# Attention value products of two key tiles by turns: four halves between changes of PSUM bank

## What is computed

```python
def _L0_attn_ref(x, query_proj, key_proj, value_proj, output_proj):
    q = jnp.einsum('bnd,hkd->bnhk', x, query_proj)
    k = jnp.einsum('bnd,hkd->bnhk', x, key_proj)
    v = jnp.einsum('bnd,hvd->bnhv', x, value_proj)
    sim = jnp.einsum('bnkh,bmhk->bnhm', q, k)
    attn = jax.nn.softmax(sim * scale, axis=1)
    o = jnp.einsum('bnhm,bmhv->bnhv', attn, v)
    return jnp.einsum('bnhv,dhv->bnd', o, output_proj)
```

## Time and profile before

| | before |
|---|---|
| median of 3 runs | 1898.89 us |
| profiled execution | 1899.13 us |
| its span | 1897.8 us |
| TensorE matmul busy | 1781.7 us (94%) |
| VectorE busy | 1708.0 us (90%) |
| ScalarE busy | 1397.8 us (74%) |
| value products (L535), time on the chain that ended last | 50% of the span |
| row maxima (L942) | 1024 of 1221 ns mean |
| exponentials (L708) | 1024 of 1113 ns mean, and 193 ns each for the row sum's read |
| value matmuls (L535) | 8192 of 614 ns mean |

### The profile page before, as it was taken

The page is one execution under the profiler, slowest core; times in us unless marked ns, Lnnn a source line. Parts: engine busy times, 40 slices in busy tenths (PEclk is TensorE's granted clock), DMA queues, the critical chain, the costliest instruction groups (busy, mean ns, idle before and its releaser), DMA issues.

```text
span 1897.8 us, 38562 instructions
## 1 busy us (share of the span) xinstructions
PE 1781.7 (94%) x15122; PEld 821.9 (43%) x15122; DVE 1708.0 (90%) x2369; ACT 1397.8 (74%) x2554; POOL 501.6 (26%) x976
## 2 busy tenths in 40 slices
PE   6969999999999999896999999999999989999996
PEld 5732222222222222581222222222222278899995
DVE  6959999999999999467999999999999789999995
ACT  3349999999999999346999999999999723222222
POOL 2002212221122112101112211221122436565664
PEclk9979999999999999997999999999999999999998
DMA  4110011110011100311111100111000222222200
GB/s 164 45 67 29 29 32 37 35 40 29 30 37 37 40 29 13 99 67 51 32 38 37 38 29 30 37 36 40 29 29 29 96 94 68 67 70 68 70 12 17
DMA packets 52980, 89.05 MB, mean 47 GB/s; under 512 B 3264, under 2 KB 35392, under 8 KB 52800
## 3 DMA queue, kind: packets, MB, share of 16 engines
q1 hardware_dynamic: 52112, 85.01, 13.9%
q10 hardware_dynamic: 688, 1.58, 0.2%
HBM read 57.21 MB, written 29.36 MB: 46 GB/s over the span
## 4 chain that ended last, share of the span: by engine, by line
PE 77%; DVE 13%; issue 3%; ACT 3%; DMA 2%; POOL 1%; SPq 0%; ACTq 0%; DVEq 0%; POOLq 0%
PE acc L535 50%; PE slot L506 11%; PE slot L390 6%; PE acc L390 5%; PE acc L552 4%; DVE nm L942 4%; ACT e_sb L708 2%; DMA stk<-qk_parts 1%; DVE e_sb L1023 1%; PE slot L593 1%; DVE ost L953 1%; DVE e_sb L1022 1%; DVE e_sb L1018 1%; DVE qx L1014 0%; DVE e_sb L1044 0%
## 5 line engine op out<-in xcount | busy, mean ns | idle before, releaser
L942 DVE TENSOR_REDUCE nm<-slot 128x1 f32<-128x1024 f32 x1024 | 1208.3, 1221 | 30.6 <-PE slot L506 25.1
L708 ACT ACTIVATE e_sb<-slot,nm 128x1024 f32<-128x1024 f32 x1024 | 1140.0, 1113 | 79.7 <-DVE nm L942 65.7
L535 PE MATMUL acc<-e_sb,vp 64*64 64x512 f32 x8192 | 1118.1, 614 | 27.8 <-DVE ost L953 15.2
L535 PEld LDWEIGHTS acc<-e_sb,vp 64*64 64x64 f32 x8192 | 228.5, 131 | 591.8 <-issue 315.1
L506 PE MATMUL slot<-stq,stk 64*64 64x512 f16 x4096 | 427.5, 385 | 36.9 <-DMA stk<-qk_parts 22.5
L506 PEld LDWEIGHTS slot<-stq,stk 64*64 64x64 f16 x4096 | 138.7, 107 | 370.9 <-ACT e_sb L708 253.4
L1169 POOL TENSOR_TENSOR dlt<-nm 128x4 f32<-128x4 f32 x128 | 25.5, 199 | 747.0 <-DVE nm L942 747.0
L708 ACT ACTIVATION_READ_ACCUMULATOR e_sb<-slot,nm 128x1 f32 x1024 | 197.4, 193 | 0.0
L1160 POOL TENSOR_TENSOR vp<-v_sb,fac 128x512 f32<-128x512 f32 x128 | 133.4, 1042 | 10.0
L791 POOL TENSOR_TENSOR hqT_lo<-e_sb,hqT_hi 128x640 fp32r<-128x640 f32 x64 | 117.8, 1861 | 50.8 <-ACT hqT_hi L642 50.8
L744 ACT COPY e_sb<-slot 128x256 f32<-128x256 f32 x32 | 11.9, 373 | 160.8 <-PE slot L563 160.8
(11 more groups left out here) (195 smaller groups left out, 1797.2 us busy)
## 6 DMA issues: line engine op xcount, KB each, us to landing
stk<-qk_parts SPq DMA_DIRECT2D x128, 128.0 KB
o_heads<-ost SPq DMA_DIRECT2D x64, 256.0 KB, 3.2
v_sb<-o_heads SPq DMA_DIRECT2D x8, 2048.0 KB, 8.3
qk_parts<-e_sb SPq DMA_DIRECT2D x32, 256.0 KB, 2.1
stq<-qk_parts SPq DMA_DIRECT2D x128, 64.0 KB
v_sb<-in_x SPq DMA_DIRECT2D x12, 512.0 KB, 9.2
out<-e_sb SPq DMA_DIRECT2D x32, 128.0 KB, 1.7
e_sb<-in_x SPq DMA_DIRECT2D x4, 512.0 KB, 10.0
```

The lines of the kernel that those rows point to most:

```text
L535: mm = pe.matmul(acc[half * VD:(half + 1) * VD, c * 512:(c + 1) * 512], vp[rows, g % 3, gi, half, :], e_v[rows, j % ERING, n0:n0 + 512], s ...
L708: act.activation(e_v[:, j % ERING, half * 1024:(half + 1) * 1024], slot[u % 3][:, :], ACT.Exp, bias=nm[:, g % 4, i, half:half + 1], accum_ ...
L942: dve.tensor_reduce(nm[:, g % 4, i, half:half + 1], slot[u % 3][:, :], AX.X, ALU.max, negate=True).then_inc(maxed.sem)
```

## The change

`attend` takes the value products of two key tiles together, in four steps: step 0 is one half of tile 2p, step 1 the half of tile 2p+1 with the same bank for each row tile; in step 2 the row tiles change banks and the other half of tile 2p follows, step 3 is that of tile 2p+1. The next pair begins with the banks that step 3 had. So the one wait of TensorE for its own earlier work is in step 2, for step 1. `attended` of tile 2p is signalled at the end of step 2, a step later than before; that of tile 2p+1 where it was. The wait for `vp` stands once for four tiles. Each step has the matmuls of a turn before.

```diff
-        def attend(b, j, turn):
+        def attend(b, n):
+            pair, step = divmod(n, 4)
+            j = 2 * pair + step % 2
+            last = step >= 2
             h, i = divmod(j, NT)
             g, gi = divmod(j, GROUP)
-            if turn == 0:
+            if step == 0 and gi == 0:
                 pe.wait_ge(*vp_made.past(b * JG + g))
-            if turn == 0 and i == 0 and h:
+            if step == 0 and i == 0 and h:
                 pe.wait_ge(*took_low.past(b * H + h - 1))
                 pe.wait_ge(*took_high.past(b * H + h - 1))
...
-            if turn == 1:
-                pe.wait_ge(*half_attended.past(b * JT + j))
-            elif j:
-                pe.wait_ge(*attended.past(b * JT + j - 1))
+            if step == 2:
+                pe.wait_ge(*half_attended.past(b * JT // 2 + pair))
             for side in range(2):
-                c = turn ^ side
+                c = (pair + last + side) % 2
                 rows = slice(side * 64, side * 64 + 64)
                 for half in range(2):
                     n0 = half * 1024 + c * 512
                     mm = pe.matmul(acc[half * VD:(half + 1) * VD, c * 512:(c + 1) * 512], vp[rows, g % 3, gi, half, :],
-                                   e_v[rows, j % ERING, n0:n0 + 512], start=(i == 0 and turn == 0),
-                                   stop=(i == NT - 1 and turn == 1))
-            mm.then_inc((attended if turn else half_attended).sem)
+                                   e_v[rows, j % ERING, n0:n0 + 512], start=(i == 0 and not last),
+                                   stop=(i == NT - 1 and last))
+            if step == 1:
+                mm.then_inc(half_attended.sem)
+            if last:
+                mm.then_inc(attended.sem)
...
-                            attend(b, j - LAG, half)
+                            attend(b, 2 * (j - LAG) + half)
```

More of the change, by code:

```diff
@@ L509, in scores @@
             mm.then_inc(scored.sem)
-        def attend(b, j, turn):
+        def attend(b, n):
+            pair, step = divmod(n, 4)
+            j = 2 * pair + step % 2
+            last = step >= 2
             h, i = divmod(j, NT)
             g, gi = divmod(j, GROUP)
-            if turn == 0:
+            if step == 0 and gi == 0:
                 pe.wait_ge(*vp_made.past(b * JG + g))
-            if turn == 0 and i == 0 and h:
+            if step == 0 and i == 0 and h:
                 pe.wait_ge(*took_low.past(b * H + h - 1))
                 pe.wait_ge(*took_high.past(b * H + h - 1))
-            elif turn == 0 and i == 0:
-                last = len(uses[b]) - 1
-                for t in range(last - 3, last + 1):
+            elif step == 0 and i == 0:
+                final = len(uses[b]) - 1
+                for t in range(final - 3, final + 1):
                     if t % 4 >= 2:
                         pe.wait_ge(*quarter_read(b, t))
-            if turn == 1:
-                pe.wait_ge(*half_attended.past(b * JT + j))
-            elif j:
-                pe.wait_ge(*attended.past(b * JT + j - 1))
+            if step == 2:
+                pe.wait_ge(*half_attended.past(b * JT // 2 + pair))
             for side in range(2):
-                c = turn ^ side
+                c = (pair + last + side) % 2
                 rows = slice(side * 64, side * 64 + 64)
```

## The result

The changed kernel takes 1830.83 us (median of 4 runs, 1828.42 to 1833.94) against 1899.7 us for the kernel before (median of 4 runs): a ratio of 0.9641, 95% interval 0.962 to 0.9662. The forecast was 1831. The profiled execution took 1828.42 us, span 1827.1 us.

What follows compares the result with a forecast made beforehand. TensorE was taken as the bound at 1.22 us a unit, VectorE next at 1.151. Units, heads' ends and tails gave 2 x (34.4 - 4.8 + 4.5) = 68.2 us off 1899.13: 1831 us, range 1823 to 1853.

Steps and rivals of the forecast that it cites:

- The bound before: In the attention stage of the kernel before, TensorE sets the pace at 1.22 us a unit.
- The third rival: The gap between value turns isn't the wait's at all, so the change does nothing: 1899 us; chance 5%.
- The sum of 1.10 us for TensorE: Units with scores and value products: 3 x 1.08 + 1.17 = 4.41 us for four, or 1.10 a unit.
- The second rival: In value steps, weights aren't loaded ahead behind scores, so TensorE stays the bound at 1.17 us: 1848 us; chance 20%.
- a wait with price 0: TensorE's rarer wait for scaled values is for something made tiles earlier, so it was priced at 0.
- VectorE as the new bound, at 1.151: In units with both, VectorE becomes the bound at 1.151 us in place of 1.22: gain 34.4 us a batch.
- The end of a head: VectorE idles 0.5 us, not 1.02, before its copy; each end costs 1.10 where it cost 0.78: -4.8 us a batch.
- The first rival: VectorE bounds but still idles 1.02 us at each head's end: 15.6 us more, 1847 us; chance 18%.
- The tail: Value products after the last maximum end 12.3 us after it in place of 16.8: gain 4.5 us a batch.
- The ring: The later `attended` signal of even tiles stays covered by 0.3 us for ScalarE's exponentials: price 0.
- The prediction's case of a unit too late (1982): In the ring, a signal one unit (1.15 us) late costs 0.37 us a pair: 1982 us; slower was given 5%.
- the later expectation (1893): Made for `after_ring_late`, not in the prediction: signal 0.45 us too late, 248 pairs x 0.25 = 62 us, 1893 us.

Runs made afterwards that it cites:

- after_wait_each: The changed kernel with its order of steps and banks, but each step waits for the step before, as each turn did: 1870.5 us, ratio 0.9846.
- after_vp_each: The changed kernel, but each step waits for the scaled values (`vp`) of its four tiles, a wait long met: 1827.5 us, ratio 0.9623.
- after_pool_small: The changed kernel with VectorE's cut of the differences and reciprocal moved to GpSimd, nothing left out: 1814.73 us, ratio 0.956 to the kernel before.
- after_max896: The changed kernel with VectorE's row maximum over 896 of the 1024 columns: 1790.98 us, ratio 0.9441 to the kernel before.
- after_ring_late: The changed kernel, but ScalarE's exponential of an even tile waits for both tiles of the pair eight tiles back: 1925.47 us, ratio 1.0138.

## Why the prediction was right

**The bound before.** Right. With its waits TensorE set the pace at 1.22 us: cutting an eighth of VectorE's maxima gave 4 us there, most of it at the heads' ends, and cutting TensorE's waits 30 and then 40. The third rival, no gain at all, is out with the result.

**The waits removed.** The sum of 1.10 us for TensorE (measured 4.39 / 4 = 1.10) held, and with it that weights are loaded ahead once no wait holds them back. The rule of the Trainium skill weighed there (TensorE: Matmul & The Clock Gate, Part 3, The mechanism, the section ahead of the one that the prediction names) says that weight loads overlap matmuls in flight only where the row group differs. It doesn't hold here: eight loads at 411.45 run for 0.37 us beside scores on the same row groups. The background buffer that the prediction cites from Part 2 of the page would fit these rows, which don't show where the weights are kept. The second rival, TensorE at 1.17, is out; `after_wait_each` shows what it would have been, a pace of 1.18 for turns with one wait (1.17 was taken from a turn that stood behind one with two) and 1870 us, not 1848, as that kernel has a second wait in every eighth unit besides. What the prediction didn't say is that the change has two parts with a price each: the waits for `vp`, 30 us when taken alone, and those for TensorE's own work, 40 on top of that. The sum treated the first as a wait with price 0. As a cost of the new kernel that was right (`after_vp_each`); as a part of the old kernel's 1.27 us turns it was counted, but not named: the prediction put those turns down to waits for the turn before alone. Its total doesn't suffer, since dropping TensorE's own waits takes both away.

**VectorE as the new bound, at 1.151.** Right, and shown from two sides: less work in the maxima gave 40 us where 41 were worked out, and the small operations moved away gave 16 where 19 were.

**The end of a head.** The direction was right, the size of one term not. The idle time was put at 0.5 and measured 0.32. The step that missed is where scores of the second half start: two spacings of 1.13 ahead plus 1.38, -0.88. The row has them at 401.00, and VectorE's maximum ends at 402.04: -1.04. Half of the 0.16 is the reciprocal, which stands between those maxima at every head's end (399.63) and was left out: the ends of the two maxima are 402.04 - 399.71 = 2.33 apart, not 2.26. The other half is the path from a maximum's end to the scores, 401.00 - 399.71 = 1.29 and not 1.38: the exponential starts 0.04 after its maximum's end (399.75), while the sum took the 0.12 of the stage's first exponential. That is near the 0.18 by which the idle time was put too long. Over 30 heads 0.18 makes 5.4 us, about the 4.9 by which the two attention stages were quicker than worked out. The first rival, 1.02 us as before, is out.

**The tail.** 4.3 us for each, worked out 4.5. What was next late did tie: the tokens of the second batch cost nothing. After the second tail a load was late that the prediction didn't name; it looked at GpSimd's folded weights only. It cost 1.15 us, and the clock 1.7 more in this execution.

**The ring.** The step was right that it wouldn't bind, and wrong in its price. It added what is left of a late signal to each pair of tiles. The run showed a closed loop through ScalarE, the slots and TensorE, in which a unit's delay costs one whole exponential of a loop. Its price is read by walking the loop once and comparing it with the pace, 4.92 against 4.60, not from the slack of one path. The prediction's case of a unit too late (1982) and the later expectation (1893) lie on both sides of the 1925 that came.

So the total agreed to a few tenths of a microsecond by some luck: the ends of heads gave 5 us more, the projection took 3 back, and the median of the runs lies 2.4 above the profiled one.

## What to carry to other kernels

Read what an engine waits for between its own instructions, and not only its busy share: TensorE was 98% busy and still lost 0.14 of each 1.22 us to waits, most of them for its own last matmul. When two row tiles of the array must not meet in a bank, order the work so that they change places as seldom as the ring allows, and drop waits that an earlier one implies, since one that is long met costs as soon as it stands beside an unmet one. After such a gain look for the next engine by shortening each one a little: where several run at nearly one pace, as here, neither busy shares (99% and 99%) nor the chain that ended last (1%) showed it.

## What the runs showed of the hardware

- A second wait in front of a turn whose first is unmet cost 0.08 us a pair of units (1.27 + 1.16 in place of 2 x 1.18, and 30 us in all). In the tail it cost the same 0.08 us in four steps (3.83 against 3.75). A single wait that had been met cost nothing (loads 0.43 us apart in the tail with it and without it; 1827.5 against 1830.8 us in all).
- f32 weight loads of four 64x64 tiles ran beside f16 matmuls of the same four tiles (eight loads within 0.37 us from 411.45, value matmuls 0.21 us after the scores).
- A 3.4 us stretch of granted clock at 0.50 (1.2 GHz) just after the second tail made sixteen projection matmuls take 5.41 us in place of 3.72. Of five kernels whose first projection waits for its load, two had the 5.41 in their profiled execution (the changed kernel and `after_pool_small`) and three the 3.72 (`after_vp_each`, `after_max896` and `after_ring_late`). TensorE had been idle for 2.06 and 2.50 us ahead of it in those two, and for 1.39, 1.85 and 1.87 in the three, in this order. Whether the idle time sets it off was not tried.
